# Transposing transfers of x moved ahead of the stack transfers of the last two chunks

## The reference

```python
x = x + tanh(g_xattn) * mha(layernorm(x), ctx, ctx)        # 16 heads of 32
x = x + tanh(g_ffn) * ffn(layernorm(x))                    # fake-quantized, 512 -> 1408 -> 512
```

## Time and profile before

| | us |
|---|---|
| median of 3 runs | 1876.84 |
| lowest and highest run | 1876.76, 1880.82 |
| the profiled execution | 1872.88 |
| its span, first to last instruction | 1871.1 |
| PE busy | 1641.4 (88%) |
| VectorE busy | 1287.6 (69%) |
| ScalarE busy | 849.4 (45%) |
| mean granted clock of TensorE | 0.951 |

### The profile page before, as it was taken

How to read it: one execution, slowest core, us unless ns; L and a number is a source line. 1 busy time by engine, 2 the same in 40 slices (tenths; PEclk the granted TensorE clock), 3 DMA queues, 4 the chain that set the end, 5 groups by cost and what they waited for, 6 DMA issues and landing times.

```text
span 1871.1 us, 34140 instructions
## 1 busy us (share of the span) xinstructions
PE 1641.4 (88%) x11832; PEld 772.2 (41%) x11880; DVE 1287.6 (69%) x2055; ACT 849.4 (45%) x1132; POOL 520.8 (28%) x782
## 2 busy tenths in 40 slices
PE   3859999889899899898988989965599999989787
PEld 2324444434444344343443444432344444434333
DVE  6627677676776676766756677566787778778555
ACT  2223524425335244252342533425777777756242
POOL 6114324234134142341432423201100000007644
PEclk7979999999999999999999999987799999989998
DMA  6445555555465455554644545324244553016897
GB/s 186 122 123 117 131 134 132 121 139 124 107 148 124 120 130 130 136 121 103 135 123 129 132 109 123 91 84 158 81 169 172 219 198 130 23 46 252 340 419 280
DMA packets 271900, 274.05 MB, mean 146 GB/s; under 512 B 157232, under 2 KB 206384, under 8 KB 269232
## 3 DMA queue, kind: packets, MB, share of 16 engines
q1 hardware_dynamic: 271792, 272.47, 50.2%
HBM read 125.84 MB, written 62.39 MB: 101 GB/s over the span
## 4 chain that ended last, share of the span: by engine, by line
SPq 30%; issue 30%; PE 19%; DMA 10%; POOL 5%; DVE 3%; ACT 2%; POOLq 0%; ACTq 0%; DVEq 0%
SPq L366 15%; SPq L345 7%; SPq L354 7%; PE bank L1308 5%; DMA x<-out_dram 4%; PE bank L1209 3%; DMA stacks<-mT 3%; PE bank L1211 3%; PE bank L1210 3%; POOL yh L612 3%; PE spair L1290 3%; DMA xT<-xl 2%; ACT pr L655 1%; DMA hb<-in_L_ffn_w_gate_dram 1%; PE bank L1200 1%
## 5 line engine op out<-in xcount | busy, mean ns | idle before, releaser
L903 DVE TENSOR_REDUCE mx<-spair 128x4 f32<-128x1024 f32 x256 | 301.4, 1219 | 57.4 <-PE spair L1265 56.9
L655 ACT ACTIVATE pr<-spair 128x1024 f32<-128x1024 f32 x256 | 258.5, 1020 | 140.5 <-PE spair L1290 140.5
L881 DVE SCALAR_TENSOR_TENSOR parts<-bank,bqk,parts 128x512 f16<-128x512 f32 x128 | 95.9, 750 | 211.2 <-ACT parts L644 208.6
L1290 PE MATMUL spair<-stacks 128*128 128x256 f16 x1024 | 157.6, 282 | 40.5 <-DMA stacks<-mT 30.1
L1406 PE MATMUL spair<-xqT,wgT 128*128 128x512 bf16 x684 | 179.3, 381 | 2.6 <-ACT xqT L767 1.6
L1406 PE MATMUL spair<-xqT,wuT 128*128 128x512 bf16 x691 | 179.9, 381 | 0.7
L644 ACT ACTIVATE parts<-bank,bqk 128x512 f16<-128x512 f32 x128 | 88.0, 687 | 201.4 <-PE bank L1211 201.4
L1308 PE MATMUL bank<-pr,v 128*32 128x256 f32 x2048 | 143.9, 400 | 28.1 <-DVE o L897 24.8
L522 POOL TENSOR_TENSOR cl<-cbuf,ch 128x512 f16<-128x512 f32 x64 | 77.2, 1210 | 287.6 <-ACT ch L632 287.6
L750 ACT ACTIVATE sil<-spair,gsc 128x512 f32<-128x512 f32 x176 | 118.2, 680 | 75.0 <-PE spair L1406 75.0
L1209 PE MATMUL bank<-xT,wqT 128*128 128x512 f16 x256 | 102.2, 399 | 56.4 <-DMA xT<-xl 54.3
(11 more groups left out here) (172 smaller groups left out, 3251.7 us busy)
## 6 DMA issues: line engine op xcount, KB each, us to landing
stacks<-parts SPq DMA_DIRECT2D x768, 64.0 KB, 2.0
x<-out_dram SPq DMA_DIRECT2D x32, 1024.0 KB, 11.0
h_spill<-hb SPq DMA_DIRECT2D x10, 2816.0 KB, 9.2
hb<-h_spill SPq DMA_DIRECT2D x10, 2816.0 KB, 15.3
xbuf<-in_x_dram SPq DMA_DIRECT2D x16, 1024.0 KB, 6.2
cbuf<-in_ctx_dram SPq DMA_DIRECT2D x16, 1024.0 KB, 6.0
xres<-in_x_dram SPq DMA_DIRECT2D x16, 1024.0 KB, 5.7
out_dram<-xres SPq DMA_DIRECT2D x16, 1024.0 KB, 6.9
```

Source lines behind the costliest of these rows:

```text
L655: act.activation(pr[:, u % 4, :, :, :].rearrange("p a b q -> p (a b q)"), spair[u % 2][:, :, :].rearrange("p a q -> p (a q)"), ACT.Exp, sc ...
L903: dve.tensor_reduce(mx[:, h:h + 2, b, :], spair[u % 2][:, :, :].rearrange("p a (q k) -> p a q k", q=KH), AX_X, ALU.max).then_inc(max_done, 1)
L1290: last = pe.matmul(spair[u % 2][:, a, kh * S:kh * S + S], kst[:, h, b * S + kh * P:b * S + kh * P + P], qst[:, h, b * S:b * S + S], start= ...
```

## The change

`turn_x(i + 1)` is called ahead of `stack(i, j, 2)` and `stack(i, j, 3)`, no longer behind them. The waits inside each stay as they are.

```diff
                 if more > 1:
                     load_c(i + 2)
+                if more > 0:
+                    turn_x(i + 1)
                 stack(i, j, 2)
                 stack(i, j, 3)
-                if more > 0:
-                    turn_x(i + 1)
                 if more > 1:
                     load_x(i + 2)
                 store_x1(j)
```

## The result

The changed kernel took 1886.2 us in the median of 6 runs (1883.68 to 1889.5), the kernel before 1878.53 in 6 (1876.76 to 1882.39). The ratio is 1.0039, with a 95% interval of 1.0024 to 1.0055: 4.5 to 10.3 us slower. That is small and clear of no change. The profiled execution took 1884.34 us, its span 1882.5. One run of the kernel before, among those made beside the experiments, took 2192.57 us at a mean clock of 0.745; no ratio counts it.

The account below looks back on a forecast made before the run. SP's queue was the chain that ended last, with score(0) following the x1 store's landing. 0 (SP) + 0 (behind the load) - 1 (row) + 4.5 (clock) = +3.5 us, so 1880.3 us; range 1868 to 1897.

Parts of the forecast that it names:

- What score(0) waits for: At body boundaries, the row of maxima lands about 0.2 us after the x1 store, whenever sent; xT is in neither chain.
- Rival A: At body boundaries, the row of maxima overtakes the x1 store: 33 us faster, 1843 us; chance 0.09.
- SP's work: On SP's queue, transposes and stack transfers swap places and the load of x stays at 782.9: sum 0.
- the margin for the low halves: The moved transposes need the low half of each x tile; POOL ends 3.4 us before that, so no wait.
- the price behind the load of c: Transposes of x right behind the 1 MB load of c: bounded at 0 to 0.6 us a body, taken as 0.
- rival D: Transposes slower behind the load of c: +0.6 us a body on SP's chain, +8.4, 1889 us; chance 0.09.
- The row's -1 us: At boundaries, earlier xT lets SP issue the row of maxima right behind the store: -1 us in all.
- The clock: PE's two pauses become one before score(0), with 11 of 14 boundaries cold at 0.9 us, six before: +4.5 us.
- rival C: Long cold starts from score(0), at clock 0.5, at 12 boundaries: 2.0 us each, +18.6, 1895 us; chance 0.11.
- Rival B: Half clock falls into PE's pause and is over by score(0): 1870.4 us; chance 0.09.
- What the profile was to show: PE's wait for xT 54.3 to about 22 us, for the row 30 to about 65; row 0.2 us behind store.
- forecast case: At boundaries, the wait for xT goes and nothing is won: own range 1876 to 1887 us, chance 0.62.

Follow-up runs that it names:

- e3: Changed kernel with the row of maxima issued ahead of the load of x and the store of x1; 1797.58 us, 0.9591 of the kernel before.
- e5: Changed kernel with the load of x right behind the transposes of x, ahead of stacks 2 and 3; 1844.04 us, 0.9825 of the kernel before.
- e6: Changed kernel with the transposes of x between the stack transfers of chunks 2 and 3; 1.0049 of the kernel before.
- e8: The changed kernel run again unaltered; 1.0048 of the kernel before.
- e2: Changed kernel with 20 added matmuls between qk(1) and score(0), their results overwritten; 1.0012 of the kernel before.
- e7: Changed kernel with 12 added matmuls between qk(1) and score(0); 1.0037 of the kernel before.
- e4: Kernel before with the row of maxima issued ahead of the load of x and the store of x1; 1837.86 us, 0.9821 of the kernel before.
- e1: Changed kernel with qk(0) held until the last x1 tile of the body before is done; 1.0049 of the kernel before.
- e10: Kernel before with the load of x between stacks 2 and 3, transposes of x still behind both; 1863.44 us, 0.9895 of the kernel before.

## Why the prediction was right

*What score(0) waits for.* Right, and the step on which all hangs. In all 15 boundaries of both kernels' profiles the row lands 0.2 to 0.3 us behind the store, with one exception of 1.0 us in the kernel before. e3 and e5 show that it is the order and not a latency: take both megabytes away and it lands in 2.2 us, take one away and it is 4.1.

*Rival A,* the row overtaking the store, is out: issued 0.4 to 1.1 us behind it at all 14 boundaries, it never did.

*SP's work, the margin for the low halves, the price behind the load of c (rival D).* Right at 0: 28.4 us for 28.5, no wait in the transposes, and e6 has the same loss with half the passing. Only the 28.8 and 29.0 of e8, e2 and e7 leave room for some tenths.

*The row's -1 us.* It came out as +0.7 in the profile, in stretches that vary by several us from body to body. It can't be told from nothing.

*The clock.* The mechanism was right, the size was not; this is the term that was mis-sized. The prediction had 11 x 0.9 - 6 x 0.9 = +4.5, and it measured +12.1 in the profiled pair. That is the rise of the 14 stretches from score(0) to the x1 tile, 0.28 us for each of the 43 us by which PE's time at half clock in the windows grew (63 us, 20 before). As the whole rest is near 0, it is about +7.7 in the medians (4.5 to 10.3).

Two things were off. The number: all 14 boundaries went cold, and not 11. The two with the shortest landings were to stay warm, but their pauses grew as well, from 1.6 and 1.8 us to 3.2 and 2.4. The prediction had named this case, +7.2, and not taken it. And the price: a cold start that reads 0.64 to 0.69 cost 0.6 to 1.3 us, in the mean 0.8, and the 0.9 fits it. But seven of the 14 read 0.50 to 0.54, a kind that none of the 14 had shown before, and those cost 1.4 to 2.1 us, in the mean 1.7. In sum the cold starts cost 17.4 us, against 5.3 before.

So half of the boundaries were rival C's long cold starts, and C's own sign, windows at 0.50, was met at those seven. Its condition, half clock that outlasts the pause by 5 us at most boundaries, was met at eight of 14 (these seven, and one of those where the clock fell late). Rival B had a part too: at the four boundaries where the clock fell 3 us ahead, some of the half clock was spent in the pause. C's price of 2.0 was near the 1.7 measured, but it does not follow from the rows: by the working that gave the prediction its 1.7 for a window at 0.69, 5.5 us at half clock can cost up to 2.75. Twelve of these less 5.4 would be +27.6, more than the stated range holds.

*What the profile was to show.* PE's wait for xT (22.2 us), the full clock ahead of qk(0) and the row 0.2 us behind the store came as said. The wait for the row was 75.4 us and not about 65. One reading was short: the work between PE's two pauses at body 9's end was 5.5 us (783.95 to 792.15 less the wait of 2.73), with turn_max counted, and not 5.2. Nothing hangs on it.

*The forecast* of +3.5 us and "within 0.3%" was therefore about half of the effect. The time lies 6 us above the 1880.3 forecast, just inside the forecast case's own range (1876 to 1887) and well inside the range. The likeliest outcome was given as within 0.3%, at 0.57, and the ratio came out 0.39% slower, on which the prediction had put 0.30. (Its interval, 0.24 to 0.55%, reaches a little under 0.3%.) The profiled pair alone, 11.5 us apart, would have put it at 1888, outside that case's own range, so that it fell inside owes something to luck.

What is shown and what is argued: that the row waits behind the store and the load is shown by e3, e4 and e5. That the changed order costs SP nothing and that the loss sits in the stretch after the cold start is shown by the columns and by e6. That the clock makes the stretches longer is shown in the profiles: the stretch of bodies 2 to 14 is 67.2 or 67.3 us wherever it is warm, in all 12 of them, and goes back with the clock in e1 and e2. That the time goes back with it is not shown, since both kernels added a cost of their own, and by their times alone e1 and e7 look like the queue theory. Why the half clock lasts longer behind the joined pause is left open.

## What to carry to other kernels

When a wait on a transfer is to be removed, ask first whether another wait ends later at the same place. Compare the landing of what comes next with the landings of the transfers ahead of it in the same queue: where a small transfer always lands just behind a big one, its issue time is worth nothing and its place in the queue is worth all. Here that place was worth 77 us together with the early transposes, and 35 without them; alone, the early transposes cost 8. Two short pauses of TensorE joined into one long one are not the same idle time: here the joined pause, 2.4 to 6.5 us, ended at the start of the critical stretch, and all 14 of those stretches then ran in part at half clock, against six before.

## What the runs showed of the hardware

A cold start costs only where the matmuls are in the chain. In the kernel before, qk(0) ran in part at half clock after its wait for xT at six of the 14 boundaries (turn_max 4.1 to 4.3 us behind it and not 2.6), and this lay hidden behind the store. In e10 the same happened at ten boundaries and delayed the row, and with it score(0), by 1.2 to 1.7 us each. In the profiles of the kernel before and the changed one the 1 MB store landed in 4.3 or 4.4 us with no load close ahead, and in 4.4 to 8.5 behind one, mostly the longer the closer the load stood.
